# Graph attention, first stage: bias added by VectorE at the table rows, rows normalised by ScalarE, sort spread over more steps

## The reference, cut to what matters

```
xn    = layernorm(x)                              # rows of 256
xp    = (xn @ W).reshape(n, 4, 64)                # 4 heads
a_src = einsum(xp, att_src); a_dst = einsum(xp, att_dst)
alpha = leaky_relu(a_src[src] + a_dst[dst]); w = softmax of alpha over each target's edges
gat   = elu(segment_sum(xp[src] * w) + bias)
```

## Time and profile before

| what | value |
|---|---|
| median of 3 runs | 3867.27 us |
| the profiled execution | 3872.03 us, its span 3870.2 us |
| mean granted TensorE clock | 0.763 |
| busy share of the span | PE 60%, DVE 51%, ACT 31%, POOL 60% |
| first stage, start to the last node row | 0 to 375.2 us |
| POOL's scatter and the barrier | 375.5 to 509.5 us |

### The profile page before, as it was taken

The page is one execution under the profiler, slowest core; times in us unless marked ns, Lnnn a source line. Parts: engine busy times, 40 slices in busy tenths (PEclk is TensorE's granted clock), DMA queues, the critical chain, the costliest instruction groups (busy, mean ns, idle before and its releaser), DMA issues. The chain is left out here.

```text
span 3870.2 us, 45381 instructions
## 1 busy us (share of the span) xinstructions
PE 2332.2 (60%) x8235; PEld 1638.3 (42%) x8235; DVE 1980.4 (51%) x4840; ACT 1206.0 (31%) x3847; POOL 2336.4 (60%) x2430
## 2 busy tenths in 40 slices
PE   6867006666676666766667666652555554108998
PEld 3534004444444444444444444442333333107887
DVE  6474025555555555555565555653788888401111
ACT  1212023333333333333243332420555555002221
POOL 4635747777777777777777777760444444273433
PEclk7667557878788788888888888875777676558999
DMA  5534044444444444444444444431555554102111
GB/s 160 158 104 141 20 77 116 119 116 118 120 118 121 116 119 120 115 123 116 121 119 117 122 119 121 119 103 34 152 157 153 155 159 141 31 1 50 53 54 48
DMA packets 273705, 418.38 MB, mean 108 GB/s; under 512 B 85664, under 2 KB 190274, under 8 KB 273410
## 3 DMA queue, kind: packets, MB, share of 16 engines
q0 software_dynamic: 103008, 263.89, 26.8%
q1 hardware_dynamic: 170530, 153.01, 12.6%
HBM read 328.00 MB, written 88.71 MB: 108 GB/s over the span
## 5 line engine op out<-in xcount | busy, mean ns | idle before, releaser
L1131 POOL DMA_INDIRECT G<-tab_d,sidx x1632 | 1545.7, 947 | 550.3 <-issue 458.9
L1847 PE MATMUL bank<-G,ident 128*128 128x264 f32 x3264 | 983.1, 466 | 471.6 <-DVE acc L1531 252.1
L1847 PEld LDWEIGHTS bank<-G,ident 128*128 128x128 f32 x3264 | 703.4, 230 | 799.1 <-DVE acc L1531 356.7
L1531 DVE TENSOR_TENSOR acc<-acc,bank 128x264 f32 x816 | 349.7, 429 | 469.2 <-PE bank L1847 451.3
L1823 PE MATMUL bank<-kvw,shared 128*128 128x512 f32 x392 | 261.3, 802 | 276.5 <-DVE shared L1454 254.5
L1717 ACT ACTIVATE G<-G,work 128x64 f32<-128x64 f32 x1632 | 394.4, 333 | 0.1
L1691 ACT ACTIVATE bank<-shared 128x512 f32<-128x512 f32 x98 | 58.9, 601 | 1011.6 <-DVE shared L1454 1011.6
L1515 DVE TENSOR_TENSOR G<-G,bank 128x1024 f32<-128x1024 f32 x306 | 350.2, 1211 | 0.0
L657 PE MATMUL bank<-G 128*128 128x256 f32 x392 | 168.3, 604 | 211.4 <-DMA G<-xnT_d 211.4
L1454 DVE TENSOR_TENSOR shared<-bank,bkv 128x512 f32<-128x512 f32 x98 | 67.7, 691 | 370.3 <-issue 350.0
L1823 PEld LDWEIGHTS bank<-kvw,shared 128*128 128x128 f32 x392 | 84.1, 238 | 385.7 <-DVE shared L1454 296.4
(11 more groups left out here) (380 smaller groups left out, 3566.2 us busy)
## 6 DMA issues: line engine op xcount, KB each, us to landing
G<-tab_d,sidx POOLq DMA_INDIRECT x1632
accP_d<-acc SPq DMA_DIRECT2D x100, 132.0 KB, 2.3
tab_d<-acc SPq DMA_DIRECT2D x49, 260.0 KB, 2.6
acc<-x_in SPq DMA_DIRECT2D x49, 256.0 KB, 3.5
xnT_d<-acc SPq DMA_DIRECT2D x49, 256.0 KB, 2.9
shared<-xnT_d SPq DMA_DIRECT2D x49, 256.0 KB, 2.9
G<-x_in SPq DMA_DIRECT2D x49, 256.0 KB, 4.9
G<-tab_d SPq DMA_DIRECT2D x49, 256.0 KB, 5.0
```

Source lines behind the costliest of these rows:

```text
L1131: g.indirect_dma_start(out=G[:, s, t, 0:TR], out_offset=None, in_=tab_d, in_offset=bass.IndirectOffsetOnAxis(ap=sidx[:, s, t:t + 1], axis= ...
L1531: v.tensor_tensor(a, a, bank[1 + i % NSB][:, 0:ROW], ALU.add).then_inc(sum_added, 1)
L1847: last = te.matmul(bank[1 + i % NSB][:, 0:ROW], ident[:, :], G[:, s, i * IT + k, :], start=(k == 0), stop=(k == IT - 1))
```

## The change

- `project` loses the bias product: two products per block instead of three. The bias stands broadcast over 128 partitions in `gbB` (264 columns, the last 8 zero).
- VectorE no longer writes `xn`. `norm` becomes `deviations` (reciprocal, and minus mean times reciprocal), and ScalarE writes `xn` as Identity with bias and scale.
- VectorE writes `xrow` from the banks with `gbB` added (`table_rows`); ScalarE copies the 8 attention columns of both blocks to `rowN` at once (`node_rows`). The stores wait for `xr_ready`, which `table_rows` raises.
- VectorE's iteration q is now deviations(q+2), stats(q+3), table_rows(q-1), then the events. The loads keep their place in SP's order.
- `sort_nodes` and `place_nodes` are cut into four and two parts. The parts stand at iterations 24, 25, 27, 29, 31, 33, 35, 37; `list_edges(k)` at min(25 + 2k, 48).
- One operation on `stat` in the node stage goes, since `deviations` has done it.

```
-            def norm(q):
-                dve.wait_ge(x_std, q + 1)
-                Chain(dve, vnm, q)(v.reciprocal(stat[:, 2 * q:2 * q + 2, 1], var[:, q % 2, 2:4]))
-                if q >= 2:
-                    dve.wait_ge(xn_T, q - 1)
-                for t in (0, 1):
-                    last = v.tensor_scalar(xn[:, q % 2, t, :], xin[:, q % 4, t, :], ..., ALU.subtract, ALU.mult)
-                last.then_inc(xn_ready, 1)
+            def deviations(q):
+                dve.wait_ge(x_std, q + 1)
+                two = stat[:, 2 * q:2 * q + 2, :]
+                Chain(dve, vnm, q)(v.reciprocal(two[:, :, 1], var[:, q % 2, 2:4]))
+                v.scalar_tensor_tensor(two[:, :, 0], two[:, :, 0], -1.0, two[:, :, 1], ALU.mult, ALU.mult).then_inc(ns_ready, 1)
+
+            def table_rows(q):
+                dve.wait_ge(tab_out[q % 2], 16 * (q // 2) + 16)
+                if q >= 2:
+                    dve.wait_ge(row_ready, q - 1)
+                for t in (0, 1):
+                    dve.wait_ge(xp_ready, 2 * q + t + 1)
+                    last = v.tensor_tensor(xrow[:, q % 2, t, :], bank[4 + 2 * (q % 2) + t][:, 0:ROW], gbB, ALU.add)
+                last.then_inc(xr_ready, 1)
...
             def store(q, s, tick):
-                settled(sp, row_ready, tick + 1)
+                settled(sp, xr_ready, tick + 1)
...
+            for at, f in ((0, degrees), (1, keys), (3, count_keys), (5, place_nodes), (7, rank_keys), (9, positions),
+                          (11, item_ends), (13, item_blocks)):
+                events.setdefault(SORT_AT + at, []).append((f, None))
             for k in range(NGB):
-                events.setdefault(min(28 + 3 * k // 2, NP - 1), []).append((list_edges, k))
+                events.setdefault(min(25 + 2 * k, NP - 1), []).append((list_edges, k))
...
             for q in range(NP):
-                if q + 1 < NP:
-                    norm(q + 1)
-                if q + 2 < NP:
-                    stats(q + 2)
+                if q + 2 < NP:
+                    deviations(q + 2)
+                if q + 3 < NP:
+                    stats(q + 3)
+                if q:
+                    table_rows(q - 1)
+                if q + 1 == NP:
+                    table_rows(q)
...
+            def norm(q):                                        # ScalarE
+                act.wait_ge(ns_ready, q + 1)
+                if q >= 2:
+                    act.wait_ge(xn_T, q - 1)
+                for t in (0, 1):
+                    last = a.activation(xn[:, q % 2, t, :], xin[:, q % 4, t, :], ACT.Identity,
+                                        bias=stat[:, 2 * q + t, 0:1], scale=stat[:, 2 * q + t, 1:2])
+                last.then_inc(xn_ready, 1)
+
+            def node_rows(q):
+                act.wait_ge(xr_ready, q + 1)
+                a.copy(rowN[:, 2 * q:2 * q + 2, W:W + NV], xrow[:, q % 2, :, D:ROW]).then_inc(row_ready, 1)
...
+            for q in range(NP):                                 # ScalarE
+                if q + 2 < NP:
+                    norm(q + 2)
+                if q + 1 < NP:
+                    turned(q + 1)
+                if q + 3 < NP:
+                    std(q + 3)
+                if q:
+                    node_rows(q - 1)
+            node_rows(NP - 1)
...
             def project(q, s):
                 pe.wait_ge(xt_ready, q + 1)
                 for t in (0, 1):
-                    xp = bank[4 + 2 * s + t][:, 0:ROW]
-                    te.matmul(xp, ones[0:1, :], gb_row[0:1, :], start=True, stop=False)
                     for k in (0, 1):
-                        last = te.matmul(xp, xt[:, s, k, t * P:t * P + P], wcat[:, k, :], start=False, stop=(k == 1))
+                        last = te.matmul(bank[4 + 2 * s + t][:, 0:ROW], xt[:, s, k, t * P:t * P + P], wcat[:, k, :], start=(k == 0), stop=(k == 1))
                     last.then_inc(xp_ready, 1)
...
-                    pe.wait_ge(row_ready, q - 1)
+                    pe.wait_ge(xr_ready, q - 1)
```

More of the change, by code:

```diff
@@ L68, in gps_kernel @@
     HT = 4
-    SORT_AT = 25
+    SORT_AT = 24
     DUMMY = float(NPAD)
@@ L178, in gps_kernel @@
         x_in = [sem(f"x_in{s}") for s in range(4)]
-        vnm, gb_ready = sem("vnm"), sem("gb_ready")
+        vnm, xr_ready, ns_ready = sem("vnm"), sem("xr_ready"), sem("ns_ready")
         x_var, x_std, xn_ready, xn_T, xt_ready, xp_ready, row_ready = (
@@ L244, in gps_kernel @@
         wmean = gpiece(48)
-        gb_row = gpiece(ROW)
+        gbB = gpiece(ROW)
         cntw = gpiece(2 * GB * P).bitcast(I32).rearrange("p (a b e) -> p a b e", a=2, b=GB)
@@ L567, in node_dve @@
             lk = Chain(dve, vns)
-            lk(v.scalar_tensor_tensor(stat[:, :, 0], stat[:, :, 0], -1.0, stat[:, :, 1], ALU.mult, ALU.mult))
             lk(v.tensor_scalar(stat[:, :, 1], stat[:, :, 1], 1.0, None, ALU.add))
@@ L990, in _ @@
             sp.dma_start(attb[:, 1, :], att_dst.rearrange("h c -> (h c)")[None, :].to_broadcast([P, D])).then_inc(ld_w, 16)
-            sp.dma_start(gb_row[0:1, 0:D], g_bias[None, :]).then_inc(ld_w, 16)
+            sp.dma_start(gbB[:, 0:D], g_bias[None, :].to_broadcast([P, D])).then_inc(ld_w, 16)
             def load_x(q, s):
@@ L1212, in _ @@
                 lk(v.tensor_reduce(wcat[:, c, D:ROW], wtmp.rearrange("p a (h n) -> p (a h) n", h=HG), AX, ALU.add))
-            v.memset(gb_row[0:1, D:ROW], 0.0).then_inc(gb_ready, 1)
+            lk(v.memset(gbB[:, D:ROW], 0.0))
             v.memset(pr_end, -1)
@@ L1292, in degrees, with keys @@
                 v.sem_inc(ix_dve, 1)
-            def sort_nodes():
+            def keys():
                 dve.wait_ge(ix_pe, 2)
@@ L1305, in sort_nodes, with count_keys @@
                                    iota_w[:, 0:KB, None].to_broadcast([P, KB, NB]), ALU.is_equal))
+            def count_keys():
                 lk(v.tensor_tensor_scan(csum, oneh, oneh, 0.0, ALU.add, ALU.max))
@@ L1334, in place_nodes, with rank_keys, positions @@
                 v.sem_inc(ix_dve, 1)
+            def rank_keys():
+                c3 = csum.rearrange("p (k b) -> p k b", b=NB)
                 lk(v.tensor_tensor(c3, c3, kbase[:, :, None].to_broadcast([P, KB, NB]), ALU.add))
                 lk(v.tensor_tensor(csum, csum, oneh, ALU.mult))
+            def positions():
                 lk(v.tensor_reduce(rsF, csum.rearrange("p (k b) -> p b k", b=NB), AX, ALU.add))
@@ L1405, in _ @@
             stats(1)
-            norm(0)
+            deviations(0)
+            stats(2)
+            deviations(1)
             for q in range(NP):
-                if q + 1 < NP:
-                    norm(q + 1)
                 if q + 2 < NP:
-                    stats(q + 2)
+                    deviations(q + 2)
[5 more added lines that the diff above has]
+                    table_rows(q)
                 if q == 1:
@@ L1637, in _, with std @@
             a = nc.scalar
-            def std(q, s):
+            def std(q):
                 act.wait_ge(x_var, q + 1)
-                a.activation(var[:, s, 2:4], var[:, s, 0:2], ACT.Sqrt).then_inc(x_std, 1)
-            def turned(q, s, u):
-                act.wait_ge(xn_T, q + 1)
[L1645 to L1649, removed]
-                for t in (0, 1):
[L1651 to L1666, removed]
+                a.activation(var[:, q % 2, 2:4], var[:, q % 2, 0:2], ACT.Sqrt).then_inc(x_std, 1)
+            def norm(q):
[6 more added lines that the diff above has]
+                last.then_inc(xn_ready, 1)
@@ new lines, in turned @@
+            def turned(q):
+                act.wait_ge(xn_T, q + 1)
+                act.wait_ge(xt_out[q % 2], 16 * (q // 2) + 16)
+                a.copy(xt[:, q % 2, :, :], bank[3][:, :].rearrange("p (k n) -> p k n", k=2)).then_inc(xt_ready, 1)
+            def node_rows(q):
+                act.wait_ge(xr_ready, q + 1)
+                a.copy(rowN[:, 2 * q:2 * q + 2, W:W + NV], xrow[:, q % 2, :, D:ROW]).then_inc(row_ready, 1)
+            std(0)
+            std(1)
+            norm(0)
+            std(2)
@@ L1667, in _ @@
+            norm(1)
+            turned(0)
+            for q in range(NP):
[8 more added lines that the diff above has]
+            node_rows(NP - 1)
             barrier(act, 1)
@@ L1791, in project @@
                 for t in (0, 1):
-                    xp = bank[4 + 2 * s + t][:, 0:ROW]
-                    te.matmul(xp, ones[0:1, :], gb_row[0:1, :], start=True, stop=False)
                     for k in (0, 1):
-                        last = te.matmul(xp, xt[:, s, k, t * P:t * P + P], wcat[:, k, :], start=False, stop=(k == 1))
+                        last = te.matmul(bank[4 + 2 * s + t][:, 0:ROW], xt[:, s, k, t * P:t * P + P], wcat[:, k, :], start=(k == 0), stop=(k == 1))
                     last.then_inc(xp_ready, 1)
-            steps = {SORT_AT: next_starts, SORT_AT + 1: bin_starts, SORT_AT + 2: block_starts, SORT_AT + 3: blocks_of_items}
```

(4 more changed lines are left out.)

3 lines of the change are left out of this document (removed).

## The result

The changed kernel took 3917.96 us (median of 5 runs, 3911.38 to 3920.15); the kernel before, run beside it, 3875.86 us (5 runs, 3865.77 to 3884.51). The ratio is 1.0107, with a 95% interval of 1.007 to 1.0145: slower by about 1.1%. The forecast was 3898 us, the range 3858 to 3925.

What follows compares the result with a forecast made beforehand. The first stage, ending with the last node rows, was taken as the bound: 59.3 start + 309.6 for 43 chains + 23.6 sort + 14 tail = 406.5 us against 375.3, 31 later, giving 3898 us, range 3858 to 3925.

Steps and rivals of the forecast that it cites:

- The end of the stage sets the time: First stage: POOL's first scatter waits for the last node rows at 375.3 us; moving that moves the time one for one.
- A closed loop through SP's stores slows the stage: First stage: table rows, two stores, x load, landing, statistics and table rows form one chain of 7.2 us a step.
- 43 chains of 7.2 us plus 23.6 for the sort: Second table rows to pair 44's rows: 43 steps, 309.6 us, plus sort parts sticking out by 23.6 us.
- the seven sort steps: VectorE's sort parts: what exceeds the 4.65 us covered by the load's wait sticks out, 23.6 us in all.
- VectorE's largest wait: First stage: the statistics wait some 4 to 5 us for the x load in nearly each of some 40 iterations.
- Start and tail: First stage's ends: second table rows end at 59.3 us; TensorE's last turns and projections take 14 us, 17 at the low clock.
- DMA by the page's fit: Load of x: the fit's 2.6 us for 256 KB gives 6.3 us a step; the trace's 3.5 us was taken instead.
- All behind is unchanged: Stages after the first scatter: their time stays the same, so the first scatter moves by as much as the total.
- A: First stage: TensorE stays the pace and statistics never wait for loads; 98 us less, 3769 us; chance 0.10.
- B: Load of x lands in 3.0 us without long gaps, chain 6.6 us; 3868 us, no change; chance 0.20.
- C: Load of x lands in 4.4 us on average, chain 8.1 us, 39 us more; 3937 us; chance 0.10.

Runs made afterwards that it cites:

- e1: The changed kernel with SyncE issuing the load of pair q+5 ahead of the two stores of pair q: 3904.8 us, ratio 1.0054 to the kernel before.
- e2: The changed kernel with ScalarE taking the root of pair q+3 before copying the transposed rows of pair q+1: 3911.41 us, ratio 1.0084 to the kernel before.
- e3: The changed kernel with both edits, load ahead of the stores and root ahead of the copy: 3823.31 us, ratio 0.9836 to the kernel before.
- e9: The kernel of e8 with four more one-column VectorE memsets just before the first barrier: 3778.28 us, ratio 0.974 to the kernel before.
- e8: The kernel of e3 with the store of the transposed rows issued once ScalarE has copied them: 3816.34 us, ratio 0.9861 to the kernel before.
- e4: The changed kernel with VectorE's table rows of pair q-1 moved to the start of its iteration: 3845.48 us, ratio 0.9892 to the kernel before.
- e10: The kernel before with 42 one-column VectorE memsets ahead of the first barrier: 3867.66 us, ratio 0.9973 to the kernel before.
- e6: The kernel before with only the sort's parts and edge lists spread to their new places: 3848.43 us, ratio 0.9939 to the kernel before.
- e11: The kernel of e8 with VectorE's table rows at the start of its iteration as well: 3812.92 us, ratio 0.9827 to the kernel before.
- e5: The kernel before, unchanged, for a second profile: 3876.13 us, ratio 1.0004; its profiled execution took 3889.21 us.
- e12: The changed kernel with four one-column VectorE memsets ahead of the first barrier, on another chip: 4975.33 us, ratio 0.9875 to the kernel before.

## Why the prediction was right, and where it was not

**The end of the stage sets the time: right.** The scatter and the barrier cost what they did (+0.2 us), and the first scatter is released by the last node rows.

**A closed loop through SP's stores slows the stage: right, but half seen.** The term "43 chains of 7.2 us plus 23.6 for the sort" was 333.2 us; measured, from the store of pair 1 to that of pair 44, 326.55. Of these the seven sort steps stick out by 23.5 us over the mean of the others (10.10, 12.91, 7.12, 12.77, 11.96, 8.51 and 9.46 against 7.05): forecast 2.9, 5.8, 0.1, 5.8, 4.9, 1.55 and 2.5, measured 3.1, 5.9, 0.1, 5.7, 4.9, 1.5 and 2.4. The ordinary step is 7.05 instead of 7.2; the x load's median landing was 3.2 us, 0.3 less than the 3.5 taken, and the two row operations took 0.77 us instead of 0.85.

What the prediction missed is that ScalarE's copy of the transposed rows waits for the same stores, and that the root stands behind it in ScalarE's order. It named VectorE's largest wait wrongly: not 4 to 5 us for the x load in some 40 iterations, but 129.6 us for the root and 9.7 for x. e1, e2 and e3 show both loops, each hidden by the other. The step that failed is the sentence "So from the end of one `table_rows` to the end of the next there is one closed chain": there were two. That the second, which had no price in the sum, is no longer than the first is luck; a longer one would have set the step, and the sum would have been wrong by the difference in each of 43 pairs.

**Start and tail.** The second `table_rows` ended at 56.96, forecast 59.3. The tail, from pair 44's rows at 383.6 to 401.1, took 17.5 us; 14 was taken, 17 was the sum by the lower clock. The granted clock in the tail was 0.70, and the turns (L1813) took 1.06, 0.60 and 0.98 us, so both levels occur. Two of ScalarE's copies still waited 3.9 us each for stores there, so a part of the excess is not the clock. The Trainium skill's rule on an array kept waiting for DMAs (TensorE: Matmul & The Clock Gate, section HAM oscillation) had pointed to the lower clock; the tail doesn't separate it from the waits. Sum for the stage: 406.5 forecast, 401.1 measured. The misses of 2.3 us at the start and 6.7 in the steps were partly made up by 3.5 in the tail.

**DMA by the page's fit.** The fit (the Trainium skill, DMA: Bandwidth & Descriptors, section Anatomy of one DMA) gives 2.6 us for 256 KB, an estimate, and with it a step of 6.3; the load took 3.2 us (median) behind two stores, and the step 7.05. The prediction was right to go by the trace. That section is on transfers which GpSimd issues, though, and this load is issued by SyncE, so the page isn't shown wrong by it.

**"All behind is unchanged": wrong.** It was the claim that the prediction itself named as its second way to fail. Half of the slowdown, 23.8 us, is in the edge stage, by VectorE's pauses at the loop's heads. That they depend on what stands ahead of the loop in VectorE's instruction stream is shown by e9, where four instructions without work, in an idle stretch, take 32.5 us off that stage. That the changed kernel's own 24 us come from the pauses rests on the agreement of sizes over the kernels of the table above, not on an edit of that kernel. What in the chip makes the pause, and which places are good, is open: 620, 662, 669 and 673 instructions ahead gave long pauses of 9.0, 9.3, 10.0 to 10.4 and 5.95 us. Without this piece the changed kernel would have been some 0.5% slower (3918 - 24 = 3894 against 3876). The forecast of the total, 3898, lies nearer to that than to the 3918 measured: the piece that was not foreseen is more than the distance between forecast and result, and moved the total to 7 us from the end of the range.

**The baseline.** One profile of before was taken for it. A second was 17 us longer in the very stage, with other clocks, while the changed kernel's five runs lie within 9 us. Against that second profile the stage lost 9 us, not 26. By the total the first profile is the nearer one to the middle: 3872.03 us, with medians of 3875 to 3878 us on its side and 3889.21 for the second. So the loss in the stage against a typical execution of before is some 22 us (an estimate: the medians differ by 42.1 us, and 20.4 of them are the other rows of the first table). The measured slowdown of 42 us is also not to be set against the forecast's 31 alone: the base rose from 3867.27 (3 runs) to 3875.86 (5 runs).

**The rivals.** A (TensorE stays the pace, 3769 us) did not happen. With the loops taken out the kernel goes part of the way, e3 and e8 to 3823 and 3816, but in e8 POOL's gathers end the stage. e9's 3778 is near A's number by the edge stage, not by A's mechanism. B and C were priced on the landing alone; it was near its median.

The best kernel is e9 at 3778.28 us, 2.6% faster than before (0.9679 to 0.9801).

## What to carry to other kernels

When a transfer's issue is made to wait for an engine, follow that engine's next iteration to the first thing that waits for the transfer: if both lie in one iteration, DMA latency is added to every step. Giving the result first and the new input second (e4) took it off here; issuing the load ahead of the stores did so only together with the second loop's edit (e1, e3). Look for every buffer that the held-up queue frees, not only for the one that you know of: two loops of equal length make each single repair look useless (8 and 10 us alone, 95 us together). And when a stage that was not edited changes by about the same amount in nearly all variants, compare its waits named `issue` before explaining it by data or clocks.

## What the runs showed of the hardware

- The same loop of VectorE pauses 5.9 and 9.0 us (before), 5.5 and 10.4 (e8), or 5.5 and 5.95 (e9) at the heads of its two chunks, by what stands ahead of it in the engine's instruction stream. Four memsets of one column moved the stage from 2082.6 to 2050.2 us.
- The kernel before, paced by TensorE in its first stage, spread from 3849 to 3904 us in 66 of 68 runs on the first chips (3910 and 3915 in the other two), e10 over 46 us in 10 runs, e6 over 19 in 12. The changed kernel stayed within 9 us in 5 runs, e1 and e2 within 11 and 19 in 10, e3, e8 and e9 within 6 in 4 each, e11 within 15 in 4. That TensorE's clock makes the difference is not shown beyond the two profiles of e5.
- On a third chip the kernel before took 30% more (5037.51 us) and e12 4975.33 us, with 1029 us more in its edge stage than e9's on another chip.
- ScalarE's Identity with scale and bias columns took 0.60 us (median) for 256 columns in the first stage, as forecast by 0.59 from another stage, and where it alternates with the root the trace has no table load (one at 0.7 us, the next at 630 us).
